# Label counts of a graph kernel: comparisons on GpSimd and row sums on VectorE in place of bf16 products on TensorE

## The reference

```python
labels = jnp.arange(1, D + 1, dtype=adj.dtype)
mask = (adj[None] == labels[:, None, None, None]).astype(dt)
weight = mask / (jnp.sum(mask, axis=-1, keepdims=True) + EPS)
agg = jnp.einsum('dbmn,bnh->bmdh', weight, hid).reshape(hid.shape[0], hid.shape[1], D * H)
out = jax.nn.relu(_linear(agg, Wd, bd))
```

## Time and profile before

| | us |
|---|---|
| median of 3 runs | 1619.71 |
| lowest and highest run | 1619.04 and 1622.42 |
| the profiled execution | 1623.08 |
| its span of instructions | 1621.3 |

### The profile page before, as it was taken

How to read it: one execution, slowest core, us unless ns; L and a number is a source line. 1 busy time by engine, 2 the same in 40 slices (tenths; PEclk the granted TensorE clock), 3 DMA queues, 4 the chain that set the end, 5 groups by cost and what they waited for, 6 DMA issues and landing times.

```text
span 1621.3 us, 44727 instructions
## 1 busy us (share of the span) xinstructions
PE 1560.4 (96%) x17424; PEld 1418.7 (88%) x17424; DVE 1311.5 (81%) x3133; ACT 1221.8 (75%) x4074; POOL 718.3 (44%) x710
## 2 busy tenths in 40 slices
PE   7899999999999999999999999999999999999986
PEld 5788999898999989989998998999899999899875
DVE  3677888888888888888888888888888888888764
ACT  4587877777787777788877778787777878777652
POOL 1344454444454444445444444544444454445321
PEclk8999999999999999999999999999999999999999
DMA  5101011110001111001111100111110011100000
GB/s 199 42 27 30 2 34 34 34 34 25 23 23 34 34 34 34 24 17 29 34 34 35 34 24 12 34 34 34 34 34 25 12 34 34 34 28 15 14 8 14
DMA packets 71426, 51.65 MB, mean 32 GB/s; under 512 B 4400, under 2 KB 69936, under 8 KB 70576
## 3 DMA queue, kind: packets, MB, share of 16 engines
q1 hardware_dynamic: 71216, 48.79, 10.0%
HBM read 40.39 MB, written 8.39 MB: 30 GB/s over the span
## 4 chain that ended last, share of the span: by engine, by line
PE 72%; ACT 20%; DVE 3%; issue 3%; POOL 1%; SPq 1%; DMA 1%; POOLq 0%; DVEq 0%; ACTq 0%
PE bank_A L404 14%; PE bank_B L404 8%; ACT E L713 6%; PE bank_B L636 6%; PE bank_A L448 5%; ACT E L777 5%; PE bank_C L404 5%; PE bank_B L448 4%; PE bank_A L636 3%; PE bank_A L422 3%; PE bank_B L416 3%; PE bank_A L434 2%; PE bank_X L557 2%; PE bank_A L532 2%; PE bank_X L568 2%
## 5 line engine op out<-in xcount | busy, mean ns | idle before, releaser
L858 POOL TENSOR_TENSOR E<-E,rsum 128x512 f32<-128x512 f32 x256 | 269.6, 1059 | 418.1 <-DVE rsum L956 285.7
L866 POOL TENSOR_TENSOR rstd<-var,minus_half 128x2 f32<-128x2 f32 x128 | 100.6, 786 | 200.5 <-DVE var L1001 200.5
L846 POOL TENSOR_SCALAR absent<-absent 128x256 int32<-128x256 int32 x64 | 55.3, 864 | 251.4 <-DMA absent<-in_adj 251.4
L1008 DVE TENSOR_SCALAR y<-y,mv,rstd 128x256 f32<-128x256 f32 x192 | 125.8, 696 | 32.8 <-POOL rstd L866 32.8
L761 ACT ACTIVATE kT<-bank_B,col 128x256 f32<-128x256 f32 x64 | 26.9, 472 | 109.4 <-PE bank_B L404 109.4
L949 DVE COPY_PREDICATED_SCALAR bank_A<-absent,fill 128x512 f32 x128 | 92.4, 743 | 12.0 <-PE bank_B L434 10.9
L404 PE MATMUL bank_A<-xT_hi,w_hi 128*128 128x256 f32 x384 | 100.4, 285 | 0.0
L404 PE MATMUL bank_A<-xT_hi,w_lo 128*128 128x256 f32 x384 | 97.5, 278 | 0.0
L713 ACT ACTIVATE E<-bank_A,nmax 128x128 f32<-128x128 f32 x256 | 91.4, 388 | 5.6 <-DVE nmax L952 5.5
L713 ACT ACTIVATE E<-bank_B,nmax 128x128 f32<-128x128 f32 x256 | 94.8, 443 | 0.0
L777 ACT ACTIVATE E<-bank_B,nmax 128x128 f32<-128x128 f32 x256 | 93.3, 418 | 0.0
(11 more groups left out here) (227 smaller groups left out, 6391.4 us busy)
## 6 DMA issues: line engine op xcount, KB each, us to landing
xt_in<-in_xt SPq DMA_DIRECT2D x64, 128.0 KB, 2.5
absent<-in_adj SPq DMA_DIRECT2D x64, 128.0 KB, 3.0
x_in<-in_x SPq DMA_DIRECT2D x32, 256.0 KB, 3.4
out<-y SPq DMA_DIRECT2D x32, 256.0 KB, 2.2
adj<-in_adj SPq DMA_DIRECT2D x32, 128.0 KB, 2.5
adjT<-in_adjt SPq DMA_DIRECT2D x32, 128.0 KB, 2.2
stage<-in_weights SPq DMA_DIRECT2D x3, 1024.0 KB, 10.6
row<-in_rows SPq DMA_DIRECT2D x1, 1024.0 KB, 7.4
```

Source lines behind the costliest of these rows:

```text
L858: nc.gpsimd.tensor_tensor(e, e, rs[:, part].unsqueeze(2).to_broadcast([P, SB, P]), ALU.mult).then_inc(e_sig.sem, 1)
L866: nc.gpsimd.tensor_tensor(rstd[part][:], var[part][:], minus_half[:], ALU.pow)\
L1008: a = nc.vector.tensor_scalar(y[part][:, g, :], src[g], mv[part][:, g, 0:1], rstd[part][:, g:g + 1], ALU.subtract, ALU.mult)
```

## The change

- `cnt` moves from TensorE to GpSimd: four comparisons of `adj1` with labels 1 to 4 into the bf16 tile `has_label`, in the place of `ne1@1`, for round n-1.
- `deg@2` is new on VectorE, behind `rec1@2`: one sum over the innermost axis of `has_label`, 1024 elements of a partition to 8 counts.
- `guard` moves from lag 4 to lag 2 at the same place of the order and reads SBUF. `degree` has four buffers, since the counts are ready about two periods ahead of `rcnt@4`.
- `wtb` is gone from ScalarE, and the eight products from TensorE.
- `ne1` moves to lag 0, behind `e0.1` and in front of `pow.2@3`, half a period earlier for its round.
- `ld_adj.1` on SP also waits for `compared`. `lab.0` waits for the `sum` of the round before in place of `guarded`; `rcnt` also waits for the accumulations of the round before.
- `ones` and its memset are gone, and a gap in SBUF shrinks from 40 to 24 elements.

```diff
     "tensor": [
...
-        "z@5 p0.3@1 p1@2 p2.0@3 cnt@4 hop0.0@1 hop0.1@1 o1@2 back0.0@1 back0.1@1 mixt@5 p2.1@3 hop0.2@1 hop0.3@1",
...
+        "z@5 p0.3@1 p1@2 p2.0@3 hop0.0@1 hop0.1@1 o1@2 back0.0@1 back0.1@1 mixt@5 p2.1@3 hop0.2@1 hop0.3@1 p2.2@3",
...
     "scalar": [
...
-        "q2@3 split.5@3 split.6@3 acc.0@5 wtb@4 hi1@2 t1@2 split.3@2 lab.2@5 exp2.0@3 lab.3@5 exp0.0@1 g1@2 exp2.1@3",
+        "q2@3 split.5@3 split.6@3 acc.0@5 hi1@2 t1@2 split.3@2 lab.2@5 exp2.0@3 lab.3@5 exp0.0@1 g1@2 exp2.1@3",
...
     "gpsimd": [
-        "e2.0@3 e0.3@1 e1@2 e2.1@3 e2.2@3 e2.3@3 pow.3@5 pow.1@2 ne1@1 absent.0 pow.0@1 sc.3@5 sc.0@1 absent.2@2",
-        "sh.0@1 sh.3@5 e0.0 sc.1@2 sh.1@2 e0.1 pow.2@3 e0.2",
+        "e2.0@3 e0.3@1 e1@2 e2.1@3 e2.2@3 e2.3@3 pow.3@5 pow.1@2 cnt@1 absent.0 pow.0@1 sc.3@5 sc.0@1 absent.2@2",
+        "sh.0@1 sh.3@5 e0.0 sc.1@2 sh.1@2 e0.1 ne1 pow.2@3 e0.2",
     ],
     "vector": [
...
-        "rec0.2@1 fill2.2@3 fill2.3@3 max2.2@3 rec0.3@1 l1w@1 rec1@2 split.4@2 gate@5 rec2.1@3 sum@5 max2.3@3",
-        "split.5@3 rec2.2@3 nrm.2@4 mixa@5 mixb@5 mixc@5 rec2.3@3 back0.0@1 back0.1@1 y1@2 bn.3@5 guard@4 agg.3@5",
+        "rec0.2@1 fill2.2@3 fill2.3@3 max2.2@3 rec0.3@1 l1w@1 rec1@2 deg@2 split.4@2 gate@5 rec2.1@3 sum@5 max2.3@3",
+        "split.5@3 rec2.2@3 nrm.2@4 mixa@5 mixb@5 mixc@5 rec2.3@3 back0.0@1 back0.1@1 y1@2 bn.3@5 guard@2 agg.3@5",
...
+                        if part == 1:
+                            wait_before(sp, compared, it, 1)
...
+                if step == "cnt":
+                    wait(pool, adj_loaded[1], it, 16)
+                    wait_before(pool, counted, it, 1)
+                    for d in range(LABELS):
+                        a = nc.gpsimd.tensor_scalar(has_label[:, :, d, :], adj1[:], float(d + 1), None, ALU.is_equal)
+                    a.then_inc(compared.sem, 1)
...
+                if step == "deg":
+                    wait(dve, compared, it, 1)
+                    nc.vector.tensor_reduce(degree[it % COUNTS][:], has_label[:], AX_X, ALU.add)\
+                        .then_inc(counted.sem, 1)
```

More of the change, by code:

```diff
@@ L216, in gnn_program @@
         nT = sb("nT", [P, NC, GN])
-        wT_b = sb("wT_b", [P, G, LABELS, P], BF16)
-        ones = sb("ones", [P, 2], BF16)
-        degree, rcnt = sb("degree", [P, G, LABELS]), sb("rcnt", [P, G, LABELS])
+        has_label = sb("has_label", [P, G, LABELS, P], BF16)
+        degree = [sb(f"degree_{u}", [P, G, LABELS]) for u in range(COUNTS)]
+        rcnt = sb("rcnt", [P, G, LABELS])
         y = [sb(f"y{L}", [P, G, D]) for L in range(4)]
         xn = [sb(f"xn{L}", [P, G, D]) for L in range(2)]
-        sb("gap_2", [P, 40])
+        sb("gap_2", [P, 24])
         xT_hi = [sb(f"xT_hi{L}", [P, NC, GN], F32R) for L in range(4)]
@@ L277, in gnn_program @@
         o2, z2_hi, z2_lo, z2_back = (signal(n, G) for n in ("o2", "z2_hi", "z2_lo", "z2_back"))
-        masked, wtb_ready, counted, guarded, rcnt_ready = (signal(n, 1) for n in ("masked", "wtb_ready", "counted",
-                                                                                  "guarded", "rcnt_ready"))
+        masked, compared, counted, guarded, rcnt_ready = (signal(n, 1) for n in ("masked", "compared", "counted",
+                                                                                 "guarded", "rcnt_ready"))
         labelled, xw_hi_ready, xw_lo_ready, agg_t = (signal(n, SB) for n in ("labelled", "xw_hi_ready", "xw_lo_ready",
@@ L615, in _ @@
                     transpose_y(A3, y[2]).then_inc(n_t[3].sem, 1)
[L616 to L623, removed]
                 if step == "lab":
@@ L627, in _ @@
                         wait(pe, xlo_ready[3], it, 1)
-                        wait(pe, guarded, it, 1)
+                        wait_before(pe, summed, it, 1)
                     if part == 1:
@@ L791, in _ @@
                                          ACT.Copy).then_inc(z2_hi.sem, 1)
[L793 to L798, removed]
                 if step == "acc":
@@ L902, in _ @@
             for t in mv:
-                nc.vector.memset(t[:, :, 2], LN_EPS)
-            nc.vector.memset(ones[:], 1.0).then_inc(consts, 1)
+                a = nc.vector.memset(t[:, :, 2], LN_EPS)
+            a.then_inc(consts, 1)
             def x0(it):
@@ L1062, in _ @@
                     a.then_inc(masked.sem, 1)
+                if step == "deg":
+                    wait(dve, compared, it, 1)
+                    nc.vector.tensor_reduce(degree[it % COUNTS][:], has_label[:], AX_X, ALU.add)\
+                        .then_inc(counted.sem, 1)
                 if step == "guard":
                     wait(dve, counted, it, 1)
-                    count = B3[:, 0:2 * G * LABELS].rearrange("p (g d two) -> p g d two", g=G, d=LABELS)
-                    nc.vector.tensor_scalar(degree[:], count[:, :, :, 0], DEG_EPS, None, ALU.add)\
-                        .then_inc(guarded.sem, 1)
+                    d = degree[it % COUNTS]
+                    nc.vector.tensor_scalar(d[:], d[:], DEG_EPS, None, ALU.add).then_inc(guarded.sem, 1)
                 if step == "rcnt":
                     wait(dve, guarded, it, 1)
-                    nc.vector.reciprocal(rcnt[:], degree[:]).then_inc(rcnt_ready.sem, 1)
+                    wait_before(dve, first_sum, it, G)
+                    wait_before(dve, summed_up, it, G * (LABELS - 1))
+                    nc.vector.reciprocal(rcnt[:], degree[it % COUNTS][:]).then_inc(rcnt_ready.sem, 1)
                 if step == "xlo":
```

1 line of the change is left out of this document (added), and 4 rows, old and new, of the table ORDER.

## The result

| | before | after |
|---|---|---|
| median of 8 runs each, us | 1621.64 | 1626.01 |
| lowest and highest, us | 1619.04, 1622.58 | 1623.33, 1628.12 |
| the profiled execution, us | 1623.08 | 1625.32 |
| its span, us | 1621.3 | 1623.5 |

The ratio is 1.0028, with an interval from 1.0018 to 1.0037, so +4.5 us (+2.9 to +6.0). I had forecast +2.3 us and "no change" as the likeliest case. By my own line of 0.2% the kernel is slower, though the lower end of the interval lies just inside the line. The time of 1626.01 us lies 4.0 us above my 1622.0, outside the range 1621 to 1623.2 that I gave the forecast; 1.9 us of that is the median of before, 1619.71 in the first three runs and 1621.64 in eight.

What follows compares the result with a forecast made beforehand. Waits at meeting points between engines, not TensorE's 96% busy time, were taken to bound the kernel. The terms, 28 x 0 + 2.2 at the start + 0.1, gave +2.3 us: 1622.0 us, own range 1621 to 1623.2, full range 1612 to 1631.

Steps and rivals of the forecast that it cites:

- e0: GpSimd steps, not a run; in round 1 e0.2 was forecast at 62.0 to 63.0 us, e0.3 at 63.0 to 64.05.
- no change: Case of a time within 0.2% (3.2 us) of the kernel before; chance 0.50.
- The products leave TensorE: Before hop0.0: the eight products run inside its wait for ScalarE's eviction L719, so removing them gains 0; bounds 0 and 7 us.
- The rival of the slot: Before hop0.0: the 0.25 us of the products' slot that was not waiting come through, -7 us, 1615 us; chance 0.13.
- The copy leaves ScalarE: ScalarE before L810: removing the 1.05 us copy only lengthens the 0.29 us wait for TensorE to about 1.2; 0.
- The sum enters VectorE: VectorE behind rec1: a sum of 1.22 us, slot 1.14, costs 0; no cost up to a slot of about 1.35.
- The comparisons enter GpSimd: GpSimd at layer 1's old mask place: four comparisons, 0.9 us each, end 5 us ahead of the transfer; cost 0.
- The rival of the port: Comparisons hold VectorE's nrm.1 and back0.4, hop0.6 late by 0.41 us a period, 11.5 us, 1633.5 us; chance 0.17.
- The mask step in the steady period: GpSimd behind e0.1: the moved step and pow.2 end at 846.1, before e0.2 at 847.79; cost 0.
- The mask step at the start: Second period: GpSimd waits for adj1's load until 60.9 us, making e0.2, e1 and TensorE's hop0.0 late; +2.2 us, once.
- e1: GpSimd step queued behind e0.3, not a run; in round 1 forecast to end about 66.7 us in place of 65.0.
- the rival of the clock: TensorE nearly empty from 59.8 to 63.1 us, clock falls to 0.50: 2 us more, up to 4; chance 0.13.

Runs made afterwards that it cites:

- The kernel without counts: Kernel before without the eight products and the copy to bf16, aggregation divided by a fixed 16; 0.9987 of before, 1622.31 us.
- the new order: Changed kernel with adj1 loaded early; ScalarE's p0.3 eviction ahead of z@5, hop0 evictions ahead of exp2.3, VectorE's rec2.3 behind back0.1; 0.9984, 1622.12 us.
- the doubled sum: Changed kernel with VectorE's sum over has_label done twice, the first into an unread tile; 1.0182 of before, 1653.55 us.
- the load forward: Changed kernel with SP issuing adj1's load right behind layer 0's adjacency load, mask step still at lag 0; 0.9989 of before, 1623.00 us.
- The kernel kept busy: Changed kernel with 44 instead of 17 dummy transposes on TensorE ahead of p0.2 of round 1; 1.0035 of before, 1629.97 us.
- the mask step back in place: Changed kernel with layer 1's mask step back at lag 1 behind the four comparisons, new counts kept; 0.9995 of before, 1623.22 us.
- the mask transfer forward: Kernel before with SP's load for absent.0 (layer 0's mask) ahead of the load that waits for VectorE's comparisons; 1.0001 of before, 1624.60 us.
- the new order in the old kernel: Kernel before, products and copy kept, with the same changed order on ScalarE and VectorE; 1.0003 of before, 1626.28 us.
- both transfers forward: Changed kernel with SP's loads for absent.0 and adj1 both ahead of the one waiting for VectorE's comparisons; 1.0007 of before, 1624.74 us.

## Why the prediction was right in its parts and short in its sum

**The products leave TensorE: 0, right.** The idle time before the weight load became 0.56 us (forecast: about 0.45) and is still ended by the same eviction. The kernel without counts puts the upper bound at 3.6 us instead of 7. The rival of the slot fell. With the new order hop0.0 did come earlier, but what the slot itself was worth there was 0.08 us of the 0.25.

**The copy leaves ScalarE: 0, right.** The wait before `xw_hi` is 1.23 us, as forecast (1.2).

**The sum enters VectorE: 0, right.** The instruction took 1.20 us (1.22 forecast) and its slot 1.12 (1.14). Shifted by 3.03 us the gate is at 803.85 (803.97) and `sum@5` at 804.63 (804.76). The bound of the slot was 1.35; the doubled sum gives 1.12 + 0.27 = 1.39 or somewhat more.

**The comparisons enter GpSimd: 0, right.** 0.865 us each (0.9). The rival of the port did not appear: nrm.1, back0.4 and hop0.6 kept their places. Its threshold of 0.92 us per comparison was not reached, so no run tested what happens above it.

**The mask step in the steady period: 0, right.** From gate to gate the kernel is not slower, and with the load forward and the mask step still in its new place it is at 0.9989.

**The mask step at the start: +2.2 us forecast, 4.2 measured. This is the step that failed, in its size.** Its first half held: the transfer was there at 60.82 (60.9), e0.2 ran from 61.87 (62.0), and e1 ended at 66.52 (66.7). What I assumed of the order fell the other way: `split.4` got the port ahead of e0.3, at 62.75, and e0.2 and e0.3 together took 4.09 us. That alone did not cost more at e1, since e1 then ran alone in 0.61 us. That e1's end came out right, from a wrong order of the three steps, is luck. The error that counts lay behind it, on TensorE. By the rows above, measured from the scores:

- e1 ends late. With p1 right behind it at about 66.55 and hop0.0 0.36 us later, as before, hop0.0 would be at 66.9 instead of 65.42, 1.5 us. With the scores 0.2 us earlier that is +1.7 us, the lower end of my 1.7 to 2.8. This is worked out from rows, not run by itself.
- The nine dummies. Before, they ran from 62.93 in the wait for e1, which lasted 0.98 us beyond them. After, they begin at 66.91, when e1 is ready. With the 1.79 us from p0.3 to hop0.0 at the full clock, hop0.0 would be at 66.01 + 1.79 = 67.8: +0.9 us. The prediction counts them only in the rival of the clock; in the forecast they cost nothing, as if they still ran inside a wait. That they were on the path is shown by the run without them.
- The low clock. From p0.3 to hop0.0 it took 3.39 us instead of 1.79: +1.6 us. This is the rival of the clock ("2 us more, up to 4"), to which I gave 0.13. Its sign, a granted clock of 0.50 between 60 and 70 us, was there; and its time with the forecast's 2.3 us makes 4.3 us at least, close to the +4.5 measured.

1.7 + 0.9 + 1.6 = 4.2 us. The kernel kept busy agrees: with p0.3 at the full clock and the dummies not, from p0.3 to hop0.0 it took 2.75 us (67.95 to 70.70), and 9.4 + 2.6 + (2.75 - 1.79) = 13.0, against 12.9 measured. So at the full clock the step would have cost 2.6 us against my 2.2, and the rest is the clock. But the clock can't be put down to the late transfer alone. It fell also in the profiled executions with the mask step back in place, the load forward, no counts, the mask transfer forward and the new order in the old kernel, none of which has the wait; it did not fall in those of before, of both transfers forward and of the new order in the new kernel.

Against its own kind, the new kernel with the transfer in time, the late transfer cost more than against the kernel before, because the gain at e1 is lost too. At the full clock, with both transfers forward, hop0.0 comes 8.2 us after the scores and not 9.4. So the late transfer costs 1.2 + 2.6 = 3.8 us at the full clock. With a low clock in both executions, the kernel after is compared with the load forward, best at the products behind the hops (L572), since in the latter a part of the low clock lies behind hop0.0:

```profile
67.08 1.13 PE L572 MATMUL bank_X<-vnat,PT 128*128 128x256 f32 x4
```

They come 14.7 us after the scores in the kernel after (70.52 - 55.81) and 10.8 with the load forward (67.08 - 56.25), 3.9 us apart. The fall of the clock is the difference between the latter and both transfers forward, 9.2 us (65.85 - 56.64): 1.6 us. 3.9 + 1.6 = 5.5 us. The ratios of the runs give 0.0033 to the mask step back in place and 0.0039 to the load forward, 5 and 6 us, in separate sets of runs. How often the clock falls in a typical execution stays open, and with it how much of the +4.5 us is the clock.

My chances put "within 0.2%" at 0.50, on a forecast that lay 1 us from the line. The step at the start was all of the sum but 0.1 us, and everything behind it on TensorE ought to have been walked through instruction by instruction.

## What to carry to other kernels

When a step is moved earlier, walk through the first periods as well as a steady one: there its data may still be on the way, and all that is queued behind it on its in-order engine, then on the engine that this one feeds, is late for once and for good. Fillers put in front of a step to cover a wait are work like any other when the wait moves elsewhere, so cost them anew with every change of order. In this kernel a removed instruction was worth its time only where the next meeting point was waiting for it; a run that leaves the work out altogether tells the most that any replacement can bring.

## What the runs showed of the hardware

- **The SBUF port between GpSimd and VectorE.** Two-operand steps held each other off to the end here: e0.2 and e0.3, 1.04 us each when alone, took 4.09 us together beside the 2.30 us of `split.4`, which slipped in between them. The gate of 512 elements runs in 0.68 us since nothing of GpSimd's lies beside it, against a median of 0.99. The one-operand comparisons, four back to back, left the pair of nrm.1 at 0.94 us. The Trainium skill ("GPSIMD Engine Reference", Specifications) has GpSimd share its SBUF interfaces with VectorE and contend with VectorE instructions that read two SBUF inputs; the gate, which does, agrees. That a waiting instruction of the other engine gets in between two of one group is what the row of 4.09 us shows here.
- **A GpSimd step has no fixed price.** Layer 0's mask step, 0.86 us in its old place, became 1.03 us on average when its transfer came earlier and it ran at another time (the kernel with both transfers forward: 65.9 us in 64 instructions, against 55.3 before).

- **TensorE's clock.** It fell to the 1.2 GHz level in the thinly used stretch at the start of round 1 in 10 of the 13 profiled executions: between 62.0 and 65.4 us in nine, and at 68.7 us in the one with 27 more dummy transposes. All five with the late transfer are among them, and five of the eight without. Executions of one and the same kernel lay between 1620.7 and 1628.8 us in a set of 27 (the kernel before); I didn't find what makes up this spread. The scores' own start, 55.0 to 57.9 us, is a part of it that lies ahead of this stretch.
